# A third order of TensorE, ScalarE and VectorE in the neighbour stage, and four weight buffers in the convolution, of a two-layer kernel

## The reference

```python
x = x + L0(gn(x))     # patches: (b, p, 288); weight: (o, p, 288)
#   out = einsum('bpi,opi->bop', patches, weight) + bias
x = x + L1(gn(x))
#   p = pts / norm over the points;  dist = |p_n|^2 - 2 p_n.p_m + |p_m|^2
#   nn_idx = top_k(-dist, 16);  nbr = pts[nn_idx]
#   logits = leaky_relu(e_n . a_own + e_m . a_other + b, 0.1);  attn = softmax over the 16
#   agg = sum(nbr * attn);  y = [pts, agg] @ W_conv + b_conv
#   y = relu(batch_norm(y)) + pts
```

## Time and profile before

| | |
|---|---|
| three runs | 12173.79, 12179.54, 12186.09 us; median 12179.54 |
| profiled execution | 12173.41 us, span of its instructions 12171.7 us |
| busy | PE 9072.4 us (75%), DVE 10502.3 (86%), ACT 10171.9 (84%), POOL 3003.3 (25%) |
| granted TensorE clock | 0.936 of 2.4 GHz in the mean |
| stages | convolve from 203.8 (first transpose) to 1138; attend from 1544 to 12034.5 (last sum), with some steps after it |
| DMA | 480.54 MB; w_in 784 issues of 144 KB, windows 42 issues of 928 KB |

### The profile page before, as it was taken

How to read it: one execution, slowest core, us unless ns; L and a number is a source line. 1 busy time by engine, 2 the same in 40 slices (tenths; PEclk the granted TensorE clock), 3 DMA queues, 4 the chain that set the end, 5 groups by cost and what they waited for, 6 DMA issues and landing times. The chain is left out here.

```text
span 12171.7 us, 324380 instructions
## 1 busy us (share of the span) xinstructions
PE 9072.4 (75%) x114746; PEld 6462.8 (53%) x114746; DVE 10502.3 (86%) x23897; ACT 10171.9 (84%) x11576; POOL 3003.3 (25%) x1648
## 2 busy tenths in 40 slices
PE   2775567777787877777878787777777777778775
PEld 2564345555555555555555555555555555555543
DVE  1000599999999999999999999999999999999997
ACT  2332389999999999999999998999999999989986
POOL 0000022222222222222222222222222222222221
PEclk9888889999999999999999999999999999989998
DMA  9667710000000000000000000000000000000003
GB/s 153 171 165 176 253 27 17 16 17 17 16 17 16 17 13 8 16 16 17 17 16 17 17 16 17 16 17 16 17 16 4 17 16 17 17 16 17 17 4 130
DMA packets 267537, 480.54 MB, mean 39 GB/s; under 512 B 196964, under 2 KB 197348, under 8 KB 248356
## 3 DMA queue, kind: packets, MB, share of 16 engines
q1 hardware_dynamic: 261348, 407.82, 14.0%
q0 software_dynamic: 4608, 51.38, 1.2%
HBM read 353.59 MB, written 105.50 MB: 38 GB/s over the span
## 5 line engine op out<-in xcount | busy, mean ns | idle before, releaser
L820 POOL TENSOR_TENSOR masked<-masked,shares_a 128x784 f32<-128x784 f32 x1600 | 2982.6, 1864 | 7532.0 <-DVE doubts L1072 5131.4
L1066 DVE MAX8 found<-scores 128x8 f32<-128x224 f32 x11200 | 3470.8, 371 | 152.2 <-ACT scores L967 119.3
L875 PE MATMUL psum<-ident_a,masked 128*128 128x128 f32 x19200 | 2717.0, 286 | 867.0 <-ACT turned_sb L994 835.4
L875 PEld LDWEIGHTS psum<-ident_a,masked 128*128 128x128 f32 x19200 | 2428.6, 198 | 1368.8 <-issue 1368.5
L994 ACT ACTIVATE turned_sb<-psum 128x512 f32<-128x512 f32 (+1 forms) x5600 | 2953.0, 570 | 208.2 <-PE psum L873 116.9
L967 ACT ACTIVATE scores<-psum 128x1568 f32<-128x1568 f32 x1600 | 2376.9, 1486 | 665.1 <-DVE minus_top L1105 633.9
L1105 DVE CUSTOM_DVE_ANT_0 masked<-masked,scores 128x3136 f32<-128x3136 f32 x800 | 2722.0, 3403 | 0.2 <-DVE scores L1097 0.2
L979 ACT ACTIVATE masked<-masked,minus_top 128x3136 f32<-128x3136 f32 x800 | 2358.9, 2949 | 0.0
L959 ACT ACTIVATE masked<-shares_a,own 128x3136 f32<-128x3136 f32 x800 | 2328.3, 2910 | 1.0
L873 PE MATMUL psum<-ident_a,masked 128*128 128x128 f32 (+1 forms) x10400 | 1752.4, 284 | 556.6 <-ACT turned_sb L994 526.7
L873 PEld LDWEIGHTS psum<-ident_a,masked 128*128 128x128 f32 (+1 forms) x10400 | 1102.0, 139 | 1304.1 <-issue 1240.2
(11 more groups left out here) (136 smaller groups left out, 6219.6 us busy)
## 6 DMA issues: line engine op xcount, KB each, us to landing
w_in<-in_L_conv_weight_dram SPq DMA_DIRECT2D x784, 144.0 KB, 2.8
points<-unit SPq DMA_DIRECT2D x128, 392.0 KB
shares_a<-share SPq DMA_DIRECT2D x32, 1568.0 KB
windows<-xg SPq DMA_DIRECT2D x42, 928.0 KB, 11.3
xg<-padded SPq DMA_DIRECT2D x32, 406.0 KB, 17.0
table<-table_sb SPq DMA_DIRECT2D x32, 404.2 KB
rows<-table SPq DMA_DIRECT2D x32, 396.0 KB
x_in<-in_x_dram POOLq DMA_DIRECT2D x8, 1568.0 KB, 12.6
```

The source lines that it names most:

```text
L820: nc.gpsimd.tensor_tensor(m, m, shares[:, t.half, k * width:(k + 1) * width], ALU.add).then_inc(logits_ready, 1)
L875: last = nc.tensor.matmul(out, block, ident[:], start=True, stop=True)
L1066: n = step(nc.vector.max(found[:, t.par, c, :], scores[:, t.par, c * PART:(c + 1) * PART]))
```

## The change

In convolve w_in has four buffers (DEEP) and not two, each with one semaphore for the loads of SP and one for those of POOL; SP loads the first two quarters of each group and POOL the others; a reload waits for the group four back. SP's and POOL's lists are written out, with constant addresses. The windows of the next row are issued in the middle of a row, before its fourth chunk. In attend VectorE's mask follows the bars of the same tile, so that merge follows its own search; POOL's first piece waits for the mask of the tile before and its second for the merge (`doubt_ready`) of its own; TensorE and ScalarE have groups 1, 2 and 6 in other places.

```diff
+    DEEP = 4
-        w_in = enter(nc.sbuf_tensor("w_in", [P, 2, SLOTS, IN_DIM], FP32))
+        w_in = enter(nc.sbuf_tensor("w_in", [P, DEEP, SLOTS, IN_DIM], FP32))
...
+        def load_weights(engine, row, j, u, quarters, loaded):
+            first = row * W + j * (2 * SLOTS) + u * SLOTS
+            k, _ = deep(0, row % 2, j, u)
+            engine.wait_ge(turned, first + SLOTS)
+            for q in quarters:
+                at = (first + q * QN) * IN_DIM
+                engine.dma_start(w_in[C * q:C * (q + 1), k, :, :].rearrange("o s i -> o (s i)"),
+                                 weight_rows[:, at:at + SLOTS * IN_DIM]).then_inc(loaded[k], 16)
...
+            load_windows(0)
+            for row in range(QH):
+                for j in range(CHUNKS):
+                    if j == CHUNKS // 2 and row + 1 < QH:
+                        load_windows(row + 1)
+                    for u in range(2):
+                        load_weights(sp, row, j, u, (0, 1), w_loaded)
...
+            for row in range(QH):            # on POOL
+                for j in range(CHUNKS):
+                    for u in range(2):
+                        load_weights(pool, row, j, u, (2, 3), w_pooled)
...
                 if passed is not None:
-                    pool.wait_ge(barred, passed.count(1, 1))
+                    pool.wait_ge(masked_ready, passed.count(1, MASKED_FREE + 1))
...
                     if k == 1:
-                        pool.wait_ge(doubts_in, t.count(1, 1))
+                        pool.wait_ge(doubt_ready, t.count(1, 1))
...
                 if past:                     # TensorE
                     turn(past, 0)
-                    turn(past, 1)
...
                 if here:
                     add_doubts(here)
                 if past:
-                    turn(past, 2)
+                    turn(past, 1)
                 if older:
                     spread_inverse(older)
+                if past:
+                    turn(past, 2)
...
-                if older:                    # ScalarE
-                    copy_turned(older, 6)
...
                 if coming:
                     copy_scores(coming, 0, tile(1))
+                if older:
+                    copy_turned(older, 6)
...
                 if past:
                     copy_turned(past, 1)
+                    copy_turned(past, 2)
                 if older:
                     copy_inverse(older, tile(SUM_LAG + 1))
                 if coming:
                     copy_scores(coming, 1, None)
                 if past:
-                    copy_turned(past, 2)
                     copy_turned(past, 3)
...
                 if here:                     # VectorE
-                    n = search(here, 1)
-                if tile(1):
-                    mask(tile(1))
-                if here:
-                    merge(here, n)
+                    merge(here, search(here, 1))
...
                     settle_doubts(here)
                     bar(here)
+                    mask(here)
```

More of the change, by code:

```diff
@@ L153, in convolve @@
         win1 = enter(nc.semaphore("c_win1"))
-        w0 = enter(nc.semaphore("c_w0"))
-        w1 = enter(nc.semaphore("c_w1"))
+        w_loaded = [enter(nc.semaphore(f"c_w{k}")) for k in range(DEEP)]
+        w_pooled = [enter(nc.semaphore(f"c_wp{k}")) for k in range(DEEP)]
         turned = enter(nc.semaphore("c_turned"))
@@ L162, in convolve @@
         block = enter(nc.Block())
[L163 removed]
+        win_loaded = [win0, win1]
         xg_rows = xg.rearrange("c h b w -> c h (b w)")
         weight_rows = weight.rearrange("o p i -> o (p i)")
[L168 removed]
+        GROUPS_PER_LAP = 2 * W // SLOTS // DEEP
+        TURN_FREE, WT_FREE, MUL_FREE, COPY_FREE = DEEP * SLOTS, SLOTS, 2 * W * PER, 2
         def each_half(engine, body):
@@ L185, in each_half_written_out, with deep @@
                     row = t * 2 + r
-                    body(row, None, None, r, None)
+                    body(t, row, None, None, r, None)
                     for j in range(CHUNKS):
                         for u in range(2):
-                            body(row, row * W + (j * (2 * SLOTS) + u * SLOTS), j, r, u)
+                            body(t, row, row * W + (j * (2 * SLOTS) + u * SLOTS), j, r, u)
+        def deep(t, r, j, u):
+            n = (r * CHUNKS + j) * 2 + u
+            return n % DEEP, t * GROUPS_PER_LAP + (n // DEEP + 1)
@@ L192, in _ @@
         def _(sp):
-            def body(row, before, j, r, u):
-                if u is None:
-                    sp.wait_ge(multiplied, row * (W * PER) + W * PER)
-                    for k in range(K):
-                        sp.dma_start(windows[k:KC:K, r, :, :],
-                                     xg_rows[:, bass.ds(row + k, PER, QH), :]).then_inc(win_loaded[r], 16)
-                    return
-                sp.wait_ge(turned, before + SLOTS)
-                for q in range(PER):
-                    at = (row * W + j * (2 * SLOTS) + (u * SLOTS + q * QN)) * IN_DIM
-                    sp.dma_start(w_in[C * q:C * (q + 1), u, :, :].rearrange("o s i -> o (s i)"),
-                                 weight_rows[:, bass.ds(at, SLOTS * IN_DIM)]).then_inc(w_loaded[u], 16)
@@ L208, in _, with load_windows @@
-            each_half(sp, body)
+            def load_windows(row):
+                sp.wait_ge(multiplied, row * (W * PER) + W * PER)
+                for k in range(K):
+                    sp.dma_start(windows[k:KC:K, row % 2, :, :],
+                                 xg_rows[:, bass.ds(row + k, PER, QH), :]).then_inc(win_loaded[row % 2], 16)
+            load_windows(0)
[5 more added lines that the diff above has]
+                        load_weights(sp, row, j, u, (0, 1), w_loaded)
@@ L234, in turn, with body @@
                 last.then_inc(turned, 1)
-            def body(row, before, j, r, u):
+            def body(t, row, before, j, r, u):
                 if u is None:
@@ L239, in body @@
                     return
-                pe.wait_ge(w_loaded[u], (row * CHUNKS + j) * (16 * PER) + 16 * PER)
+                k_in, lap = deep(t, r, j, u)
+                pe.wait_ge(w_loaded[k_in], lap * (8 * PER))
+                pe.wait_ge(w_pooled[k_in], lap * (8 * PER))
                 for s in range(AHEAD):
-                    turn(before, s, u)
+                    turn(before, s, k_in)
                 pe.wait_ge(copied, (row * CHUNKS + j) * 2 + (u + 1))
@@ L246, in body @@
                     if s + AHEAD < SLOTS:
-                        turn(before, s + AHEAD, u)
+                        turn(before, s + AHEAD, k_in)
                     pe.wait_ge(wt_ready, before + (s + 1 + WT_FREE))
```

2 lines of the change are left out of this document (removed).

## The result

The changed kernel takes **12,332.8 us** in the median (12,322.6 to 12,361.3) against 12,176.7 for the kernel before on the same chip: ratio 1.0131, 95% interval 1.0112 to 1.015. It is slower by 156 us, where the forecast was 12,070 in a range of 11,870 to 12,230.

What follows compares the result with a forecast made beforehand. VectorE was taken to bound the neighbour stage; in the convolution no engine was full. From 12,173 us, 163 less in the convolution and 59 more in neighbour-stage waits gave 12,069, about 12,070, range 11,870 to 12,230.

Steps and rivals of the forecast that it cites:

- windows in the middle of the row: Convolution: SP's weights queue behind the next row's windows, leaving a 4.7 us TensorE wait 13 times, +61 us.
- the small waits: Convolution: waits for weights from having only two buffers, 78 us, all to go with four buffers.
- 260 us of excess: Convolution: time over 674 us of bare groups, 182 at thirteen row changes and 78 in small waits.
- Rival 3: Convolution: weight path no faster, POOL's loads late or windows and weights blocking; only 60 less, 12,178 us; chance 0.10.
- VectorE's own work: Neighbour stage: nothing removed, three changes where instructions touch cancel, leaving VectorE's step at 12.59 us.
- Lower bars: Neighbour stage, VectorE: GpSimd's second piece starts earlier and overlaps these less, -0.33 us a step.
- Links: Neighbour stage, VectorE: new dependences, sum after its bars +0.22 us and merge after its maxima +0.11 us a step.
- TensorE's idle time: Neighbour stage: TensorE sits still 3.0 us before the doubts in every step, so its clock was taken to fall.
- What that costs: Neighbour stage: slowed TensorE makes VectorE wait 0.35 us in some 370 steps, 130 us, plus 0.65 in 112, 73 us.
- X: Neighbour stage: VectorE's waits for scores and doubts, forecast 203 us, bounds 20 and 500.
- rival 2: Neighbour stage: half clock feeds itself, TensorE slow for whole steps, waits of 500 us, 12,370 us; chance 0.15.
- the sign that I had set: Neighbour stage: VectorE waiting over 330 us for scores and doubts would show that rival 2 holds.

Runs made afterwards that it cites:

- e1: Changed kernel with the convolution of the kernel before, so the neighbour stage's change alone: 12,384.8 us, 1.0173 of the kernel before.
- e4: Changed kernel without the window loads after the first two rows, multiplying old windows: convolution stage 767.4 us, whole 12,334 us.
- e7: Kernel before with one wait changed, GpSimd's second piece starting at the merge, not when the doubts are in: 12,005.5 us, 0.9859.
- e8: Changed kernel with the old orders of both TensorE and ScalarE put back: 12,128.1 us, 0.9959 of the kernel before.
- e2b: Changed kernel with four unused identity products filling TensorE's idle time before the doubts, in steps without a 1x1 product: 12,190.1 us, 1.0014.
- e9: Changed kernel with TensorE's old order alone put back: 12,406.5 us, 1.0193 of the kernel before.
- e3: Changed kernel with each row's window loads cut into twelve pieces of 232 KB, spread over ten groups: 12,304.7 us, 1.0107.

## Why the prediction was wrong

**Convolution: step "windows in the middle of the row", the term that failed.** Predicted -163, measured -43 at the next stage's start (-52 by e1, -55 for the stage itself). That the small waits and the 13 us waits for weights go was right; none of them is left. The loss left by the windows was forecast as a wait for SP's share of the weights, 61 us. No such wait came. What came was a wait that is not in my sum at all, one without a releaser, read as TensorE's code: 146 us in place of 14. The windows account for 78 of them (118 less 40, e4). Of the other 68, 54 are new as well, though they don't need the windows. Some 26 of these come where the loop comes round, and may have stood under the row's wait for weights before; no run here separates that from another cause, so their cause stays open. Of the 260 us of excess 97 were to stay, and some 205 did; the new code waits are 132 of them. Instead of 771 the stage takes some 880. Rival 3 (only 60 less: "windows and weights block one another") had the size right and another mechanism.

**VectorE's own work: right in its parts.** Lower bars -0.33 predicted, -0.34 measured (1.349 to 1.010). Links: the gap before the sum is 0.19, not 0.14, which with the lost overlap makes 2.02 from upper bars to sum where it was 1.76, +0.26 instead of +0.22. The merge starts 0.13 later, +0.11 predicted. The step is 12.64 (6010.67 to 6023.31) instead of 12.59: +0.05, 40 us that I had cancelled to nothing. The whole comes out near zero only because the early piece on GpSimd is in it: e7 and e8 put the two at -154 and +152 in the span of the sums.

Timeline of the changed kernel, the step that answers to the earlier trace rows:

```profile
6010.67 2.14 DVE L1090 MAX8 found<-scores 128x8 f32<-128x224 f32 x7
6012.85 0.28 DVE L1151 MAX8 best<-found 128x8 f32<-128x112 f32 x1
...
6014.99 0.19 PE L882 MATMUL psum<-ones,above 128*1 128x1 f32 x2 [2.95 <-DVE rest L1161]
6015.24 1.98 PE L898 MATMUL psum<-ident_a,masked 128*128 128x128 f32 x8
...
6017.94 1.83 DVE L1121 SCALAR_TENSOR_TENSOR scores<-scores,bound,shares_a 128x1568 f32<-128x1568 f32 x1
6019.96 3.42 DVE L1129 CUSTOM_DVE_ANT_0 masked<-masked,scores 128x3136 f32<-128x3136 f32 x1 [0.19 <-DVE scores L1121]
6023.31 0.08 DVE L1129 DVE_READ_ACCUMULATOR2_ANT minus_top<- 128x1 f32 x1
```

**"TensorE's idle time": right in kind, too frequent.** 3.0 us before the doubts was predicted for every step, and used in the sum for some 370 of them. It is 2.95 in the step above, but by the timeline rows only 208 of 800 steps have between 2 and 3.5 us there, 107 of them 2.5 or more. A clock of 0.87 or less was predicted, 0.87 measured; and e2b shows that the clock is what makes the scores late in this order. The Trainium skill ("TensorE: Matmul & The Clock Gate", section "HAM oscillation — how this bites in real kernels") has this pattern, a wait that comes back in each turn of a loop and lowers the clock each time; the trace agrees in part. Between 1600 and 12,000 us the changed kernel has 216 idle times of 2 to 3.5 us, counted from its timeline rows, the kernel before 16 and e2b 46. But e8 has 264 of them at a clock of 0.92, and e9 8 at 0.89: their number does not set the clock by itself, so that 0.87 was met to the digit is partly luck.

**"What that costs": the term that was mis-sized.** I let X be 203; it is 336, past the 330 that I had named for rival 2. (In e1 and e3, with the same neighbour stage, it is 301 and 312, just under.) The prediction took 370 waits of 0.35 us and 112 of 0.65; the trace has fewer and longer ones (total us, times, longest, between 1543 and 12,034 us):

```profile
DVE found L1090 <- ACT scores L991: 285.6, 217, 7.6
```

That is 1.3 us each. These two terms close the account of the stage: X is 133 over my figure and the step 40, which makes the 229 out of the 59 to within 3 us. I had worked out how late ScalarE's copy of the *same* step comes and taken off its slack once. The timeline at 6118 shows where the rest arises: the lag passes through ScalarE's exponential and bank copies to TensorE's groups of the next tile, and comes to VectorE one step later as 1.62. With ScalarE at 9,600 of 10,704 us there was little idle time to take it up. By the sign that I had set (over 330 us) rival 2 should hold, but its mechanism is not what the trace shows: in the steps at 6118 the gap closes behind the late step and the matmuls return to 0.94 and 1.06 us, and by the granted clock only 12 of the 799 steps from sum to sum are over nine tenths at half clock, as against 11 in the kernel before. TensorE is not at half clock for whole steps; this is the forecast's mechanism, priced too low.

**The chances.** Slower had 0.15. Both terms missed to the same side. A like reason suggests itself, though the runs do not prove it: each stage lost a slack that had covered something else, code in the one, ScalarE's small reserve in the other. The rivals were priced one at a time, so the range held no case with both.

**What stays open.** e9 has a clock of 0.89 with no more than 8 idle times from 2 to 3.5 us; what lowers it there was not found. Nor was it found why e8 keeps 0.92 with more idle times of 2 to 3.5 us than the changed kernel. The clock's price was measured in the changed order alone, by e2b: 240 of 311 us of late scores, 160 net of the late doubts. In the old orders e8 shows none, at 0.92. Whether the 54 us of new code waits that don't need the windows come from the wait for weights that went, or from the written-out lists, is open too.

## What to carry to other kernels

An order written out by hand on several engines is one object: put back on one engine alone it lost 74 or 207 us here, on both it was worth 205, so cost a reorder as the whole ring of who waits for whom, and follow a lag through the engine that is nearly full into the next step. Before a wait is counted as gained, ask what it may have covered: when the waits for weights went, 132 us of other waits came out, 54 of them with no windows in flight. And take the pieces of a bundle apart: one line of this change, run alone, was worth 172 us; VectorE's new order used that up, and the new orders of TensorE and ScalarE cost 205 more.

## What the runs showed of the hardware

- **TensorE's waits without a releaser grow with the data in flight.** In the multiplies they were 118 us with three window loads of 928 KB per row, 83 with twelve of 232 KB, and 40 with none, the program being otherwise the same. That they are waits for code is my reading. The instruction queues move 21 MB, 0.7% of the engines' time, in the kernel before and after alike, so if it is the code, it is its place in line and not its volume. Loads of weights in flight beside windows suffer too: SP's issued at 281.84 landed by 296.7, against a median of 3.6 us.
- **GpSimd's additions hold up VectorE's one-source bars.** Where both run at once for 0.53 us the bars take 1.37 instead of 1.04, 0.33 more; moving the additions away gave 272 us of busy time in 800 steps in e7. The kernel before has steps with other overlaps too:

```profile
2010.95 1.85 POOL L820 TENSOR_TENSOR masked<-masked,shares_a 128x784 f32<-128x784 f32 x1 [6.13 <-DVE doubts L1072]
2012.42 1.22 DVE L1096 TENSOR_SCALAR scores<-scores,bound 128x1568 f32<-128x1568 f32 x1
```
```profile
12029.95 1.85 POOL L820 TENSOR_TENSOR masked<-masked,shares_a 128x784 f32<-128x784 f32 x1 [5.89 <-DVE doubts L1072]
12031.04 1.59 DVE L1096 TENSOR_SCALAR scores<-scores,bound 128x1568 f32<-128x1568 f32 x1 [1.17 <-DVEq L1089]
```

  An overlap of 0.38 costs 0.18, one of 0.53 costs 0.33, one of 0.76 costs 0.55: each further microsecond of overlap costs a full one, less a constant 0.2. The Trainium skill ("SBUF — State Buffer", section "Terms") says that the loser on the shared ports waits until the other is done. The slope agrees with that; the size does not, by the constant 0.2, which may lie in the recorded ends of GpSimd's instructions, as these are rough in a profile. The 160 us that this rule promised beyond the sum did not come, and could not: without any overlap the bars still take 1.04.
- **Work without use can be cheap.** Four products that compute nothing, in each step without a 1x1 product (4,652 more matmul records in the stage, where each of these fp32 products shows as two), raised the granted clock of the stage from 0.87 to 0.94 and made the changed kernel 143 us faster, though no faster than the kernel before (1.0014).
